# Softmax reciprocals for two and four rows at once, and evictions of the next block moved ahead, in an attention and expert kernel on one core

## The reference

```python
h = _layernorm(x) * (1 + ca) + sa
x = x + ga * attention(h, Q_w, Q_b, K_w, K_b, V_w, V_b, O_w, O_b)
h = _layernorm(x) * (1 + cb) + sb
x = x + gb * ffn(h, Wr, router_bias, Wg, Wu, Wd, Sg, Su, Sd)

# attention
q, k, v = h @ Q_w + Q_b, h @ K_w + K_b, h @ V_w + V_b          # per head
logits = where(causal_mask, -100000, q @ k.T / sqrt(128))
out = (softmax(logits) @ v) @ O_w + O_b
```

## Time and profile before

| | |
|---|---|
| median of 3 runs | 2032.54 us (2032.47 to 2037.23) |
| the profiled execution | 2040.55 us, its span 2038.9 us |
| mean granted TensorE clock | 0.985 of full |
| PE busy | 1942.8 us (95%) |
| DVE busy | 1422.5 us (70%) |
| ACT busy | 1121.6 us (55%) |
| POOL busy | 568.8 us (28%) |

### The profile page before, as it was taken

One profiled execution on the slowest core, in us unless ns is written; L12 is line 12 of the kernel. 1 busy time (PEld: TensorE's weight loads), 2 busy tenths in 40 slices (PEclk: granted clock), 3 DMA queues, 4 the chain that ended last, 5 costly groups with the idle time before them and its releaser, 6 DMA issues.

```text
span 2038.9 us, 33861 instructions
## 1 busy us (share of the span) xinstructions
PE 1942.8 (95%) x9821; PEld 1147.9 (56%) x9821; DVE 1422.5 (70%) x3593; ACT 1121.6 (55%) x1638; POOL 568.8 (28%) x585
## 2 busy tenths in 40 slices
PE   5899999999999999999999999689999999999998
PEld 2444444444444444444444444368877778777786
DVE  5787797797797797797797797546545843333477
ACT  3576776776676676676676676413333144344311
POOL 5430330330330330330330311632000132222265
PEclk8999999999999999999999999799999999999999
DMA  6278777777777777777777777874431098999676
GB/s 237 64 173 176 172 173 176 172 173 176 172 172 176 173 172 176 178 168 176 175 171 176 172 156 160 206 207 142 124 109 32 1 294 276 314 293 312 223 209 185
DMA packets 932246, 366.68 MB, mean 180 GB/s; under 512 B 754800, under 2 KB 885920, under 8 KB 932128
## 3 DMA queue, kind: packets, MB, share of 16 engines
q1 hardware_dynamic: 921888, 331.93, 64.9%
q0 software_dynamic: 10240, 33.56, 5.3%
HBM read 138.86 MB, written 41.94 MB: 89 GB/s over the span
## 4 chain that ended last, share of the span: by engine, by line
PE 66%; DVE 8%; DMA 6%; SPq 6%; issue 6%; POOL 4%; ACT 3%; DVEq 0%; ACTq 0%; POOLq 0%
PE gen L1696 9%; PE gen L1697 9%; PE gen L1698 9%; PE strip L1696 6%; PE strip L1698 6%; PE strip L1697 6%; PE pv L1697 5%; PE pv L1696 5%; PE pv L1698 5%; SPq L500 5%; PE strip L2005 4%; DMA wd_sb<-in_L_ffn_Wd 3%; DVE p_lo L1281 2%; PE strip L2012 2%; POOL gath L887 2%
## 5 line engine op out<-in xcount | busy, mean ns | idle before, releaser
L935 ACT ACTIVATE exps<-exps,nbias,cols_now 128x128 f32<-128x128 f32 (+15 forms) x256 | 329.8, 1288 | 176.2 <-DVE cmin L1267 174.2
L1281 DVE SCALAR_TENSOR_TENSOR p_lo<-exps,rinv,p_hi 128x512 f16<-128x512 f32 (+3 forms) x256 | 404.5, 1606 | 26.2 <-ACT p_hi L944 25.2
L944 ACT ACTIVATE p_hi<-exps,rinv 128x512 f16<-128x512 f32 (+3 forms) x256 | 335.4, 1352 | 37.2 <-issue 15.7
L1257 DVE TENSOR_SCALAR_CACHE_REDUCE exps<-strip 128x512 f32<-128x512 f32 x384 | 250.9, 687 | 128.2 <-PE strip L1698 127.2
L1696 PE MATMUL strip<-kT_hi,qT_hi 128*128 128x512 f16 (+3 forms) x640 | 221.1, 350 | 30.7 <-DVE kT_lo L1210 21.6
L1696 PE MATMUL pv<-pT,v 128*128 128x512 f16 (+3 forms) x640 | 223.3, 349 | 3.5 <-DMA pT<-p_lo 3.5
L1697 PE MATMUL strip<-kT_lo,qT_hi 128*128 128x512 f16 (+3 forms) x640 | 223.6, 349 | 0.0
L1697 PE MATMUL pv<-pT,v 128*128 128x512 f16 (+3 forms) x640 | 223.3, 349 | 0.0
L1698 PE MATMUL strip<-kT_hi,qT_lo 128*128 128x512 f16 (+3 forms) x640 | 221.2, 349 | 0.0
L757 POOL TENSOR_TENSOR wq_f<-wq_f,fac 128x512 f32<-128x512 f32 x16 | 16.7, 1041 | 730.7 <-PE gen L1698 726.8
L1698 PE MATMUL pv<-pT,v 128*128 128x512 f16 (+3 forms) x640 | 219.8, 349 | 0.0
(11 more groups left out here) (266 smaller groups left out, 4309.5 us busy)
## 6 DMA issues: line engine op xcount, KB each, us to landing
at_dram<-at_f SPq DMA_DIRECT2D x64, 256.0 KB, 2.5
wg_sb<-in_L_ffn_Wg SPq DMA_DIRECT2D x64, 256.0 KB
wu_sb<-in_L_ffn_Wu SPq DMA_DIRECT2D x64, 256.0 KB
wd_sb<-in_L_ffn_Wd SPq DMA_DIRECT2D x64, 256.0 KB
yb_dram<-yb SPq DMA_DIRECT2D x64, 256.0 KB
a_f<-at_dram SPq DMA_DIRECT2D x58, 256.0 KB, 2.8
pT<-p_hi SPq DMA_TRANSPOSE x320, 2.7
pT<-p_lo SPq DMA_TRANSPOSE x320, 2.8
```

Source lines behind the costliest of these rows:

```text
L935: nc.scalar.activation(row, row, ACT.Exp, bias=nbias[:, t:t + 1], scale=cols_now[:, LOGIT_UP:LOGIT_UP + 1], accum_out=rsum[:, t:t + 1]).th ...
L944: nc.scalar.activation(p_hi16[:, 0:j + 1, t, :], row, ACT.Copy, scale=rinv[:, t:t + 1]).then_inc(p_hi, 1)
L1257: nc.vector.tensor_scalar(exps[:, t, 512 * ch:512 * ch + w], strip[u % STRIPS][:, 0:w], 1.0, None, ALU.mult, ALU.max, accum_out=cmax[:, t, ...
L1281: nc.vector.scalar_tensor_tensor(p_lo16[:, 0:j + 1, t, :], row, rinv[:, t:t + 1], p_hi16[:, 0:j + 1, t, :], ALU.mult, ALU.subtract).then_i ...
```

## The change

On VectorE `row_inverse` becomes `row_inverses`, which takes several neighbouring rows with the same two instructions. It waits until all of its rows are summed, and counts its semaphores up by as many rows.

- Stages 1 to 3: one pair of instructions for rows 0 and 1, after score row 2, and one for rows 2 and 3, after `probs_lo` of rows 0 and 1.
- Stage 0: one pair for all four rows, after score row 3.
- Stage 3: the stage's own values go out after score row 3 and no more after row 1.
- Stage 1: the next queries and keys go out between `probs_lo` of rows 2 and 3, and no more after row 3.

On ScalarE, in stage 1 alone, the next queries and keys go out before `attended`.

```diff
 ScalarE, stage()
-                if prev is not None:
+                if j == 1:
+                    gen_hi_of("q", nxt[1], nxt[0])
+                    gen_hi_of("k", nxt[1], nxt[0])
+                    attended(*prev)
+                    gen_hi_of("v", nxt[1], nxt[0])
+                elif prev is not None:
                     attended(*prev)
...
-                elif nxt is not None:
+                elif j > 1 and nxt is not None:
...
 VectorE
-            def row_inverse(h, j, t):
-                n = h * NT + (TB * j + t + 1)
+            def row_inverses(h, j, t, rows):
+                n = h * NT + (TB * j + t + rows)
                 dve.wait_ge(row_probs, n)
-                nc.vector.tensor_scalar(rsum_small[:, t:t + 1], rsum[:, t:t + 1], 1.0 / PSCALE, None, ALU.mult
-                                        ).then_inc(rsum_scaled, 1)
+                nc.vector.tensor_scalar(rsum_small[:, t:t + rows], rsum[:, t:t + rows], 1.0 / PSCALE, None, ALU.mult
+                                        ).then_inc(rsum_scaled, rows)
                 dve.wait_ge(rsum_scaled, n)
-                nc.vector.reciprocal(rinv[:, t:t + 1], rsum_small[:, t:t + 1]).then_inc(rinv_ready, 1)
+                nc.vector.reciprocal(rinv[:, t:t + rows], rsum_small[:, t:t + rows]).then_inc(rinv_ready, rows)
...
 VectorE, stage()
                 score_row(h, j, 0)
                 score_row(h, j, 1)
-                row_inverse(h, j, 0)
-                if j == QB - 1:
-                    gen_out_of("v", QB - 1, h)
                 score_row(h, j, 2)
-                row_inverse(h, j, 1)
+                if j > 0:
+                    row_inverses(h, j, 0, 2)
                 score_row(h, j, 3)
-                if j == 1:
-                    gen_out_of("v", 1, h)
+                if j in (1, QB - 1):
+                    gen_out_of("v", j, h)
                 if j == 0:
-                    row_inverse(h, j, 2)
-                    row_inverse(h, j, 3)
+                    row_inverses(h, j, 0, TB)
                     gen_out_of("q", nxt[1], nxt[0])
                     gen_out_of("k", nxt[1], nxt[0])
                     probs_lo(h, j, 0)
                     probs_lo(h, j, 1)
                 else:
                     probs_lo(h, j, 0)
-                    row_inverse(h, j, 2)
                     probs_lo(h, j, 1)
-                    row_inverse(h, j, 3)
+                    row_inverses(h, j, 2, 2)
                     if j == QB - 1:
                         take_columns(h + 1)
                 probs_lo(h, j, 2)
+                if j == 1:
+                    gen_out_of("q", nxt[1], nxt[0])
+                    gen_out_of("k", nxt[1], nxt[0])
                 probs_lo(h, j, 3)
                 if nxt is not None:
                     hn, jn = nxt
-                    if j > 0:
+                    if j > 1:
                         gen_out_of("q", jn, hn)
                         gen_out_of("k", jn, hn)
```

More of the change, by code:

```diff
@@ L1450, in _ @@
             score_row(h, j, 1)
-            row_inverse(h, j, 0)
+            score_row(h, j, 2)
+            row_inverses(h, j, 0, 2)
+            score_row(h, j, 3)
             gen_out_of("v", QB - 1, h)
-            score_row(h, j, 2)
-            row_inverse(h, j, 1)
-            score_row(h, j, 3)
             probs_lo(h, j, 0)
-            row_inverse(h, j, 2)
             probs_lo(h, j, 1)
-            row_inverse(h, j, 3)
+            row_inverses(h, j, 2, 2)
             split_a(0)
```

## The result

The changed kernel takes 2085.13 us (median of 4 runs, 2084.03 to 2087.74), the kernel before 2034.88 us (2032.47 to 2038.4) in the runs beside it: 1.0232 times as long, 95% interval 1.022 to 1.0244, which is 45 to 50 us more (the two medians are 50 us apart). Forecast were 2069 us with a range of 2047 to 2088, so 36 us more.

What follows compares the result with a forecast made beforehand. The bound was taken to be the chain from a stage's first matmul to the next low keys in stages 1 to 3. Terms +0.0 + 1.85 + 0.57 + 0.0 = +2.42 us a head, times 15, gave 2069 us, range 2047 to 2088.

Steps and rivals of the forecast that it cites:

- Stage 1: Late pairs offset attended leaving ScalarE's path: low keys at 1028.64 for 1028.65, +0.0 us; first eviction of stage 2 +0.74.
- Stage 2: Late first eviction, late pairs and a 0.44 us pair and hand-over make the third stage begin 1.85 us late.
- S: The first eviction of a stage; in stage 2 forecast at 1030.37 and not 1029.64, +0.74 us.
- Stage 3: GpSimd's product ends before the first p_lo, so 0.85 us of blocking goes; late pairs still cost, +0.57 us.
- P: A stage's first matmul, taken as set by the chain to the low keys in stages 1, 2 and 3.
- Stage 0: Three inverses removed, about 0.8 us, but PE's projection decides when the next keys go out: no gain taken.
- SyncE: Transposes of stage 2 land in time; values of stage 3 delay 0.7 us against 3 us of slack: nothing.
- 1: Stage 3: GpSimd's blocking of the first p_lo stays, +1.13 us there, 2077 us in all; chance 0.2.
- 2: Late first pairs hidden or a hand-over shorter, half of stage 2's steps go: +18 us, 2051 us; chance 0.12.
- 3: VectorE's work decides, not ScalarE's, so PE's waits come back: 23 us faster, 2010 us; chance 0.07.
- 4: Stage 1 gains 1.0 us, stages 2 and 3 lose as much: within 6 us of 2032; chance 0.06.
- 5: PE's longer waits let its clock drop to the lower level: 6 us a head, above 2095 us; chance 0.03.

Runs made afterwards that it cites:

- both counts by one: The changed kernel with the semaphores behind scaling and reciprocal each raised by one a call, not by the number of rows: 1.019 times the kernel before.
- the product moved: The changed kernel with GpSimd making b_diag some 13 us later, after the wait for the next weights' sizes: 1.023 times the kernel before.
- the last version above: Kernel before with four reciprocals at once in stage 0, next queries/keys sent earlier in stages 1 to 3, values of stages 2 and 3 after row 3: 0.9936.

## Why the prediction was right, point by point

| stage | before | forecast | measured | both counts by one |
|---|---|---|---|---|
| 1 | 14.65 | 14.65 | 14.67 | 14.36 |
| 2 | 18.89 | 20.74 | 21.04 | 20.73 |
| 3 | 24.59 | 25.16 | 25.63 | 25.47 |
| 0 | 18.97 | 18.97 | 18.97 | 18.97 |
| head | 77.10 | 79.52 | 80.31 | 79.53 |

- **What bounds it**: right. Three stages in four follow the chain to the next low keys, and it lengthened the head at once, with VectorE's work down by 2.3 us. Of the 16 us between 2069 and the measured 2085, fifteen times the missing 0.79 us a head make 11.9, and 2.3 are the higher median of the kernel before in the runs beside the changed one.
- **Stage 1**: the links came out within 0.15 us each: the keys were no sooner, PE waited its 1.0 us still, and VectorE idled 1.2 us before the third p_lo. That the sum is right to 0.02 us is in part luck. Counting by rows, which I did not know of, adds 0.31 us, and the rest of the chain is 0.29 shorter than forecast (14.36 with both counts by one). Part of that is the first two p_hi: I kept their 2.33 us of the earlier trace rows, but in it the second stood for a moment behind its own reciprocal, and behind a pair the two take 2.19.
- **Stage 2**: the mechanism right (first eviction 0.73 us later, forecast 0.74), the term mis-sized by 0.30 us. The step that failed is "pair and hand-over 0.44": it is 0.58, and the first p_hi also came 0.17 us later than forecast (S + 6.04 for S + 5.87). With both counts by one the hand-over is 0.43 and the stage 20.73, to 0.01 us what was forecast. I had bounded a two-row instruction by the nearest row, one of three columns; its length was right, but the row said nothing of a count raised by two.
- **Stage 3**: +1.04 for +0.57. "The product then ends 0.24 us before p_lo starts" came true with room to spare (it ended at 1098.06, p_lo started at 1098.70), and yet the first p_lo was blocked, because GpSimd's next product, `b_diag`, had moved up and started at 1098.60, 0.1 us ahead of it. In the kernel before that one stood behind the p_lo. I followed one instruction of the queue and not the ones behind it. Undone alone, this gives back 0.17 us a head, and counting by one gives back 0.16; 0.14 of the 0.47 us remain. They lie in how the two hide each other, since the second pair waits for the later of exponential 3 and the second p_lo. With both undone the first p_hi would start 8.65 us after P (as with both counts by one), exponential 3 end 7.95 later (as with the product moved) and the third p_hi start 0.43 after that: P + 17.03 for P + 17.52, and the stage would take 25.14 us (forecast 25.16). That is an estimate from those traces; the two were not run together. It also shows that a head of 79.53 us with both counts by one, for 79.52 forecast, is luck: its stage 1 is 0.29 us under the forecast, its stage 3 0.31 over.
- The rule of the Trainium skill ("SBUF — State Buffer", "SBUF: two separate sides") that a VectorE instruction with two SBUF inputs and a GpSimd one that reads SBUF exclude each other fits both rows: 0.85 us longer behind a product of 1.04 that had just begun, 0.52 behind one of 0.83 that began 0.1 us ahead. Both are some 0.2 us less than what was left of the product (1.03 and 0.73).
- **Stage 0**: "I take nothing for it" was slightly off. The four reciprocals at once, alone, gave some 2 us in all.
- **SyncE**: right. The first p_hi of stage 3 was released by the reciprocal and not by a transpose.
- **Last head**: its spare wait of 7.44 us shrank to 3.83. It swallowed the loss of stage 2, as forecast, and more: that stage takes 24.87 us, and took 26.97.

```profile
1328.48 0.78 ACT L950 ACTIVATE at_f<-pv,at_bias,at_scale 128x512 f32<-128x512 f32 x1 [3.83 <-issue]
```

- **Rivals**: 1 gave the nearest time (2077 us, and more was measured), but for a part of a wrong reason: the blocking's price on the path is 0.17 us and not 0.56, because exponential 3 is the later condition of the pair once the blocking goes. 2 failed on the point that was named: from the first p_hi to the end of exponential 3 ScalarE has no gap. 3 failed on its condition, since the third p_hi of stage 2 starts 2.1 us later after P than before, and 4 because stage 1 gained nothing. 5 did not come here, with waits of up to 1.7 us at full clock.

## What to carry to other kernels

Batching small instructions delays the first result to the time of the last input. Before doing it, ask who waits for the first one: here 0.5 us of VectorE's time saved in a stage cost up to 2 us, since two engines take turns on a chain and VectorE's busy share was not the bound. Work moved behind a releasing instruction comes back as a later start of the next stage, so follow each engine once round the loop before counting a gain.

## What the runs showed of the hardware

- Raising a semaphore by more than one in an instruction that also waits turned its wait into a sequencer instruction of its own, and a scaling and reciprocal of this kind held the p_hi behind them up by 0.14 to 0.19 us: 0.27 us from scaling to reciprocal for 0.21, and 0.78 us a head in all. As far as these kernels show, a count that goes up by one a call is free.
- A reciprocal of two rows takes 0.17 us and of one 0.16, so the saving in VectorE's time is real.
- A scaling of two columns that starts inside a GpSimd product ends with it (0.86 and 0.41 us for 0.17), and one of a single column is not held (0.15 us inside a product).
- A p_lo and a GpSimd product hold each other up, whichever is first: p_lo takes 3.18 or 2.87 us for 2.33 behind a product, and `b_diag` 2.75 us in the kernel before, where it starts behind a p_lo, for 0.83.
- After a wait of 2.4 us PE came back at the lower clock in four heads of fifteen and at full clock in the others (in the last version above it also did after the one wait of 2.31 us of its first head, 0.61 over the next 4.4 us); after the waits of up to 1.7 us in the changed kernel's heads between 250 and 1200 us it always came back at full clock.
